# Local attention on one Trainium2 core: inverse norms by refinement steps for two groups at once, and a new table of slots

## The reference

```python
q, k, v = jnp.split(shift_tokens(x) @ Wqkv, 3, -1)      # 16 heads of 64
q = q / jnp.maximum(jnp.linalg.norm(q, axis=-1, keepdims=True), 1e-12) * qs
k = k / jnp.maximum(jnp.linalg.norm(k, axis=-1, keepdims=True), 1e-12) * ksc
q = q * cos * scale + rotate_half(q) * sin * scale
k = k * cos / scale + rotate_half(k) * sin / scale
x = local_attention(q, k, v, window=32) @ Wo + x
x = ffn(shift_tokens(x)) + x                            # layernorm, W1, gelu gate, W2
```

## Time and profile before

| | us |
|---|---|
| median of 3 executions | 4810.02 (4803.85 to 4811.19) |
| the profiled execution | 4799.15 |
| its span | 4797.3 |
| phase B in it | about 512 to 4070 |
| busy, share of the span | PE 88%, DVE 84%, ACT 78%, POOL 73% |

### The profile page before, as it was taken

One profiled execution on the slowest core, in us unless ns is written; L12 is line 12 of the kernel. 1 busy time (PEld: TensorE's weight loads), 2 busy tenths in 40 slices (PEclk: granted clock), 3 DMA queues, 4 the chain that ended last, 5 costly groups with the idle time before them and its releaser, 6 DMA issues. The chain is left out here.

```text
span 4797.3 us, 131407 instructions
## 1 busy us (share of the span) xinstructions
PE 4226.0 (88%) x45166; PEld 3150.4 (66%) x45166; DVE 4007.1 (84%) x7658; ACT 3749.9 (78%) x11543; POOL 3518.3 (73%) x2504
## 2 busy tenths in 40 slices
PE   6988699998999989998889989999899998688887
PEld 3555477776777777776777767777677776354553
DVE  4776798888888888888888888898898895688887
ACT  2555588888888888888888888888888887677774
POOL 0100699988899888998989989899899995344444
PEclk9999799999999999999999999999999999788888
DMA  1000111111111111111111111111121111000000
GB/s 27 6 5 2 49 48 44 44 38 52 53 40 43 48 48 47 44 44 45 46 53 43 40 45 52 47 44 44 45 53 38 44 44 28 3 4 3 3 3 5
DMA packets 118641, 169.38 MB, mean 35 GB/s; under 512 B 26563, under 2 KB 44422, under 8 KB 118022
## 3 DMA queue, kind: packets, MB, share of 16 engines
q1 hardware_dynamic: 109246, 160.92, 12.7%
q10 hardware_dynamic: 8776, 0.45, 0.1%
HBM read 20.79 MB, written 2.10 MB: 5 GB/s over the span
## 5 line engine op out<-in xcount | busy, mean ns | idle before, releaser
L1377 POOL TENSOR_TENSOR b_w<-b_w,b_vt 128x512 f32<-128x512 f32 x768 | 1188.4, 1558 | 331.8 <-DVE b_vt L1289 184.1
L1381 POOL TENSOR_TENSOR b_rn<-b_ssm,all_neg_half 128x16 f32<-128x16 f32 x384 | 1171.7, 3051 | 32.0
L1174 ACT ACTIVATE b_Pr<-ps,b_nm 128x96 f32<-128x96 f32 x3072 | 1002.8, 353 | 3.4 <-DVE b_nm L1346 2.8
L1174 ACT ACTIVATION_READ_ACCUMULATOR b_Pr<-ps,b_nm 128x1 f32 x3072 | 677.1, 220 | 0.0
L1216 ACT ACTIVATE b_PT<-ps 96x512 f32<-96x512 f32 x768 | 458.1, 597 | 264.1 <-PE ps L1026 257.1
L1060 PE MATMUL ps<-b_Whi,b_xlo 128*128 128x512 f32 x1152 | 579.2, 503 | 61.7 <-DVE b_Wlo L1306 25.8
L989 PE MATMUL ps<-all_ident,b_w 128*128 128x128 f32 x3072 | 460.6, 281 | 182.3 <-DVE b_xtok L282 118.7
L1340 DVE TENSOR_TENSOR b_Pr<-b_Pr,b_rinv 128x384 f32<-128x384 f32 x768 | 547.0, 712 | 26.3
L1026 PE MATMUL ps<-all_ident,b_Pr 128*96 128x128 f32 x3072 | 479.2, 279 | 68.8 <-ACT b_PT L1216 47.1
L1287 DVE TENSOR_TENSOR b_w<-ps,until_b_rotab 128x512 f32<-128x512 f32 x768 | 524.0, 682 | 8.9 <-ACT b_sq L1193 5.4
L1346 DVE TENSOR_REDUCE b_nm<-ps 128x8 f32<-128x768 f32 x384 | 367.5, 957 | 190.8 <-PE ps L1015 184.6
(11 more groups left out here) (259 smaller groups left out, 9375.4 us busy)
## 6 DMA issues: line engine op xcount, KB each, us to landing
b_V<-b_Vraw SPq DMA_DIRECT2D x384, 192.0 KB, 2.6
b_V<-b_Vraw SPq DMA_DIRECT2D x384, 128.0 KB, 2.4
b_V<-b_Vraw SPq DMA_DIRECT2D x192, 64.0 KB
b_Wraw<-in_L_ffn_Wqkv SPq DMA_DIRECT2D x36, 256.0 KB, 3.4
b_Wo<-in_L_ffn_Wo SPq DMA_DIRECT2D x6, 512.0 KB, 4.5
a_xtok<-in_L_attn_hidden_states SPq DMA_DIRECT2D x16, 128.0 KB, 2.1
out<-c_xout SPq DMA_DIRECT2D x16, 128.0 KB, 1.8
b_W<-in_L_ffn_W SPq DMA_DIRECT2D x6, 341.0 KB, 3.3
```

What stands on the lines that cost most here:

```text
L1174: last = nc.scalar.activation(s.Pr[:, r % 2, j, i], ps[:, S_BANK[j], i * KEYS:(i + 1) * KEYS], ACT.Exp, bias=s.nm[:, r, j, i:i + 1], accum ...
L1377: nc.gpsimd.tensor_tensor(rows, rows, s.vt[:, i % 4], ALU.add).then_inc(s.pool_add, 1)
L1381: nc.gpsimd.tensor_tensor(s.rn[:, j], s.ssm[:, j], g.neg_half[:, 0:HB], ALU.pow).then_inc(s.pool_r, 1)
```

## The change

What it does:

- The clamp and the power of each group (8 instructions a step on POOL) give way to inverse_root(b), called after add 3 (b = 0, groups 0 and 1) and after add 7 (b = 1, groups 2 and 3). It is a chain of 12 instructions on both groups at once, 128x32 each: clamp and scale, a first guess from the bits of the number as an integer, and two refinement steps. Each waits for the one before it on the semaphore root_step; the last counts pool_r up, once for two groups.
- Both of DVE's groups, 2 and 3, are now normalised within the step (slots 28 and 31), POOL's two at slots 13 and 19. PE's waits for them follow the tables.
- The slots are laid anew: the pieces at 0, 4, 6, 7, 16, 18, 22, 23; ROTATE_LAG is 0 where it was 2; both halves of a round are exponentiated in one slot (lags 4, 4) and scaled in one (5, 5); the moments stand at 20, the last residual at 27, the gate product on POOL at 22.

```diff
-QK_SLOT = {0: (0, 0), 2: (0, 2), 6: (1, 0), 8: (1, 2), 16: (0, 1), 17: (0, 3), 22: (1, 1), 24: (1, 3)}
-ROTATE_LAG, ADD_LAG = 2, 2
+QK_SLOT = {0: (0, 0), 4: (0, 2), 6: (1, 0), 7: (1, 2), 16: (0, 1), 18: (0, 3), 22: (1, 1), 23: (1, 3)}
+ROTATE_LAG, ADD_LAG = 0, 2
...
-DVE_NORM_SLOT = {27: 2}
-DVE_LATE_NORM_SLOT = {4: 3}
-POOL_NORM_SLOT = {7: 0, 16: 1}
+DVE_NORM_SLOT = {28: 2, 31: 3}
+DVE_LATE_NORM_SLOT = {}
+POOL_NORM_SLOT = {13: 1, 19: 0}
...
-                    dve.wait_ge(s.pool_r, 4 * item + j + 1)
+                    dve.wait_ge(s.pool_r, 2 * item + j // 2 + 1)
...
+                def inverse_root(b):
+
+                    done = ROOT_STEPS * (2 * f + b)
+                    js = slice(2 * b, 2 * b + 2)
+                    x, y, t = s.ssm[:, js], s.rn[:, js], s.rt[:]
+                    three, linear, constant = [g.root_c[:, i].rearrange("p (j h) -> p j h", j=2) for i in range(3)]
+                    nc.gpsimd.tensor_scalar(x, s.ss[:, js], 1e-24, ROOT_S, ALU.max, ALU.mult).then_inc(s.root_step, 1)
+                    pool.wait_ge(s.root_step, done + 1)
+                    pool.sem_inc(s.root_step, 1)
+                    nc.gpsimd.tensor_scalar(y.bitcast(I32), x.bitcast(I32), -0.5, ROOT_MAGIC, ALU.mult, ALU.add).then_inc(s.root_step, 1)
+                    pool.wait_ge(s.root_step, done + 3)
+                    nc.gpsimd.tensor_tensor(t, x, y, ALU.mult).then_inc(s.root_step, 1)
+                    pool.wait_ge(s.root_step, done + 4)
+                    nc.gpsimd.tensor_tensor(t, t, y, ALU.mult).then_inc(s.root_step, 1)
...
+                    pool.wait_ge(s.root_step, done + 12)
+                    nc.gpsimd.tensor_tensor(y, t, y, ALU.mult).then_inc(s.pool_r, 1)
...
-                        if c // 2:
-                            nc.gpsimd.tensor_scalar_max(s.ssm[:, j], s.ss[:, j], 1e-24).then_inc(s.clamp_done, 1)
-                            pool.wait_ge(s.clamp_done, 4 * f + j + 1)
-                            nc.gpsimd.tensor_tensor(s.rn[:, j], s.ssm[:, j], g.neg_half[:, 0:HB], ALU.pow).then_inc(s.pool_r, 1)
+                        if i % 4 == 3:
+                            inverse_root(i // 4)
```

More of the change, by code:

```diff
@@ L13 @@
 from contextlib import ExitStack
+import math
 import numpy as np
@@ L22 @@
 F32R = mybir.dt.float32r
+I32 = mybir.dt.int32
 ALU = mybir.AluOpType
@@ L153, in _ @@
             nc.vector.memset(g.neg_half[:], -0.5)
+            for i, value in enumerate(ROOT_C):
+                nc.vector.memset(g.root_c[:, i], value)
             nc.vector.memset(g.minus[:], -1.0)
@@ L1359, in body, with normalise @@
                 f, t, u = step.n + 1, step.n - 1, step.n - 2
+                def normalise(item, j):
+                    pool.wait_ge(s.pool_r, 2 * item + j // 2 + 1)
+                    pool.wait_ge(s.pool_add, N_QK * item + 2 * j + 2)
+                    both = s.w[:, j % 2, j // 2].rearrange("p k (h e) -> p (k h) e", e=DB)
+                    nc.gpsimd.tensor_tensor(both, both, s.rn[:, j].rearrange("p (h o) -> p h o", o=1).broadcast_to((P, HB, DB)),
+                                            ALU.mult).then_inc(s.normed_pool, 1)
@@ new lines, in inverse_root @@
+                def inverse_root(b):
[11 more added lines that the diff above has]
+                    nc.gpsimd.tensor_tensor(t, t, y, ALU.mult).then_inc(s.root_step, 1)
+                    pool.wait_ge(s.root_step, done + 5)
+                    nc.gpsimd.tensor_tensor(t, three, t, ALU.subtract).then_inc(s.root_step, 1)
+                    pool.wait_ge(s.root_step, done + 6)
+                    nc.gpsimd.tensor_tensor(y, t, y, ALU.mult).then_inc(s.root_step, 1)
+                    pool.wait_ge(s.root_step, done + 7)
+                    nc.gpsimd.tensor_tensor(t, x, y, ALU.mult).then_inc(s.root_step, 1)
+                    pool.wait_ge(s.root_step, done + 8)
+                    nc.gpsimd.tensor_tensor(x, t, y, ALU.mult).then_inc(s.root_step, 1)
+                    pool.wait_ge(s.root_step, done + 9)
+                    nc.gpsimd.tensor_tensor(t, x, linear, ALU.subtract).then_inc(s.root_step, 1)
+                    pool.wait_ge(s.root_step, done + 10)
+                    nc.gpsimd.tensor_tensor(t, t, x, ALU.mult).then_inc(s.root_step, 1)
+                    pool.wait_ge(s.root_step, done + 11)
+                    nc.gpsimd.tensor_tensor(t, t, constant, ALU.add).then_inc(s.root_step, 1)
+                    pool.wait_ge(s.root_step, done + 12)
+                    nc.gpsimd.tensor_tensor(y, t, y, ALU.mult).then_inc(s.pool_r, 1)
@@ L1360, in body @@
                 for slot in range(STEP_SLOTS):
                     if step.front is not None and slot in POOL_NORM_SLOT:
[L1362 to L1367, removed]
+                        normalise(f, POOL_NORM_SLOT[slot])
@@ L1368, in body @@
+                    if step.attn and slot in POOL_LATE_NORM_SLOT:
+                        normalise(step.n, POOL_LATE_NORM_SLOT[slot])
                     if step.front is not None and slot - ADD_LAG in QK_SLOT:
```

41 lines of the change are left out of this document (26 added, 15 removed).

## The result

The changed kernel takes 4978.83 us (median of 4 runs, 4977.92 to 4980.03) against 4807.07 of the kernel before on the same chip: ratio 1.0356, 95% interval 1.0344 to 1.0369, 172 us slower. The forecast was slower, 4900, in a range from 4765 to 5015.

The account below looks back on a forecast made before the run. The loop through DVE was taken to set the pace, 35.7 us a step. The new loop, 36.05 + 0.7 = 36.75, adds 1.1 over 84 steps: 92 on 4799, plus 11, gives 4900 us, range 4765 to 5015.

Parts of the forecast that it names:

- The loop: DVE's group 2 product waits for rotate 7, add 7 and the chain: 36.0 or 36.1 us a step, against 35.7.
- under 3 us a step, the chain's links were cheaper: Sign of being wrong: DVE's wait for rn before the product in normalise that small means cheaper links.
- 30.5 us from group 2's product round to the end of rotate 7: DVE's own part of the loop, into the next step: 31.9 - 1.4 = 30.5 us.
- The two extra terms: On top of the loop: waits for round 1's exponentials, 0.5 us a step, and POOL late at rotate 7, 0.2.
- The collisions at 1.4 us: DVE's scalings and products slowed opposite POOL's work: kept at 1.4 us a step, bounds 0.5 and 2.0.
- 84 steps, two at the change of layers swallow it: About two of a layer's 16 steps absorb the loss, leaving 14 x 6 = 84 steps, 92 us.
- What the other moves cost: at nothing: The other moved slots cost nothing, as PE needs 33.1 us of a 36.75 us step.
- worth nothing by itself: POOL's 5.4 us a step less work gains nothing, since others did not wait for POOL.
- The gelu in the way: Gelu at slot 22 on ACT delays rotate 7 in odd steps: up to 84 us more, 4985; chance 0.12.
- The dear chain: POOL's chain takes 5.6 us instead of 4.1: 126 us more, 5025; chance 0.12.
- the integer instruction that costs like a power: In POOL's chain it costs some 5.5 us on 32 columns: 437 us more, 5340; chance 0.04.
- The faster rival: Links of 0.28 us, fewer collisions: 4776 or 4701; decided by chain plus extra terms under 3.7 us; chance 0.2.

Follow-up runs that it names:

- new_slots_product: Changed kernel's slot table without chains, each group's clamp kept and its power replaced by a product, norms not computed: 4875.12 us (1.0146).
- short_second: Changed kernel with only the second chain (groups 2 and 3) cut from twelve to six instructions: 4850.06 us (1.0088).
- chain_alone: Kernel before with its old slots but the two chains; POOL's product for group 0 moves from slot 7 to 12: 5303.51 us (1.1035).
- old_slots_product: Kernel before with its power on POOL replaced by a product of the same shape, norms not computed: 5062.58 us (1.0533).

## Why the prediction was right in its direction and half in its size

**The loop: right.** Its link was to be the product of group 2 waiting for add 7 and the chain. The wait is there once a step, the second chain takes 4.03 against 4.1 (the first, opposite DVE's splits, 4.7), and taking half of it out where it stands in the loop gives back 129 us, against 6 elsewhere. The signature "about 4 us" came as 2.9, since 1.8 of the gap carries PE's name, as the working had said of the last residual. So the sign "under 3 us a step, the chain's links were cheaper" was met and pointed wrong: the links were 0.33, as priced.

**"30.5 us from group 2's product round to the end of rotate 7": mis-sized, and the largest part of the miss.** Measured 31.25 (2074.39 to 2105.64), and 31.66 in the step before it, with the 0.3 for a square in it. It is not that DVE works more, its busy time is the same. The 31.9 it was worked out from subtracts 7.5 us of waits from the pair, and one of the four waits for scores in the earlier trace rows had passed before the pair's window begins, at 2174.74. DVE in the kernel before:

```profile
2172.22 0.56 DVE L1340 TENSOR_TENSOR b_Pr<-b_Pr,b_rinv 128x384 f32<-128x384 f32 x1
2174.38 0.96 DVE L1346 TENSOR_REDUCE b_nm<-ps 128x8 f32<-128x768 f32 x1 [1.60 <-PE ps L1015]
```

The pair itself holds 7.5 - 1.6 = 5.9 us of waits. DVE's own time was thus (71.36 - 5.9)/2 = 32.7 a step, small gaps included, and the loop's term 31.3. The changed kernel gives the same 32.7, worked out with its 9.6 us of waits: (74.95 - 9.6)/2.

**The two extra terms: the sum nearly right, by luck, the shares not.** The exponentials of round 1 were to cost 0.5; DVE waits 1.8 us for them in all of 1000 to 3500, so nothing. POOL was to be 0.2 late; it is 0.5. With these the working reads 31.3 + 1.3 + 0.08 + 4.03 + 0.08 + 0.5 = 37.3, plus 0.15 for the square of piece 23 (0.3 once a pair) 37.4, against 37.47 measured.

**The collisions at 1.4 us: right in sum.** The scaling's mean rose from 710 ns to 745 in 1000 to 3500, the first half of the split from 303 to 688, the product's fell from 1.35 to 1.22, so (8 x 0.185 + 2 x 0.01) is 1.5 a step by the forecast's way of counting; the new meeting of add 1 and the scaling of round 0 that was foreseen takes 1.66 instead of 0.56.

**"84 steps, two at the change of layers swallow it": wrong.** Over one whole layer of 16 steps, before and after (the converting step and the fourth after it beneath):

```profile
1655.25:2246.10 590.85, 538.52 (x6562) 428.56 (x6561) 517.85 (x1031) 506.67 (x1678) 524.38 (x337) 0.99 0.17 46
1655.25:1702.98 47.73, 37.22 (x413) 28.57 (x412) 37.02 (x71) 34.36 (x109) 33.05 (x22) 0.93 0.18 49
1810.53:1852.59 42.06, 36.04 (x413) 28.80 (x412) 32.93 (x65) 31.22 (x103) 33.05 (x23) 0.92 0.23 64
```

```profile
1710.05:2328.06 618.01, 548.34 (x6563) 433.92 (x6560) 518.88 (x1031) 510.54 (x1679) 386.34 (x593) 0.98 0.17 44
1710.05:1760.83 50.78, 37.93 (x411) 29.12 (x408) 37.76 (x72) 33.88 (x109) 24.89 (x39) 0.87 0.17 45
1874.22:1915.73 41.51, 36.96 (x410) 28.81 (x408) 32.91 (x66) 31.19 (x103) 24.17 (x38) 0.92 0.22 61
```

27.2 us a layer, 163 in six. The converting step pays 3.05 itself, and only the one of 42.06 swallows the change. The two errors make the miss on the whole: 92 us were forecast as 84 x 1.1; 96 x 1.1 is 106, and 96 x 0.7 = 67 more for the mis-sized step gives 173, against 172. Why the converting step got longer though DVE came later wasn't tried; the granted clock in it fell from 0.93 to 0.87, and whether that is a cause of it is open.

**"What the other moves cost: at nothing": right for the forecast, too kind on POOL's time.** The cover that was named does hold in the changed kernel, since the chain's wait hides the rest: the last residual is done 2.4 and 3.3 us ahead of rn. What the new order costs with no chain stays open, since the 68 us of new_slots_product have a meeting of POOL and DVE in them that the changed kernel hasn't. And "worth nothing by itself" for POOL's freed time (8.5 us a step in busy time in 1000 to 3500, 5.4 in the forecast, which counted the gaps in the chains) was too kind: in the old order a kernel whose POOL has some 10 us less to do is 256 us slower.

**The rivals.** The gelu in the way is refuted: the square of piece 23 waits 0.3 us in odd steps, and the steps are 37.22 and 37.73. The dear chain is refuted, and so is the integer instruction that costs like a power: 0.22 us. The faster rival is refuted at its first condition, a link of 0.28: it is 0.33. Its point of decision, chain and extra terms under 3.7 us, is refuted too: in short_second the second chain has lost six links of 0.33, so chain and lateness come to some 2.5, and the kernel is still 0.9% slower than before. DVE's own time is 0.8 us a step higher than reckoned, and in every second step of short_second its way to rotate 7 is another 1.5 us longer, mostly by waits for ACT. By the slope of the Trainium skill (GPSIMD Engine Reference, section 3.1) the chain would have taken 2.5 us, an estimate; the trace doesn't agree, with 4.03.

**What fell of my theory.** The loop sets the time of the changed kernel, but it is not DVE's alone. Five rearrangements that were to take the wait off DVE's queue, or hide work in it, lost or gave little (5404, 5301, 5226, 5707, 4932), as other waits took its place. What they share, as I read them, is that groups 2 and 3 are finished last and needed first; pairing them makes group 2 wait for rotate 7. A second cause isn't separated from this: in the four slow ones and in chain_alone the granted clock over the run is 0.90 to 0.93 where it is 0.96 before and after, and PE is busy 35.3 to 36.7 us a step in 1000 to 3500 instead of 34.3, so part of their loss may be slower work on PE. No version beat the kernel before. How much of the 5304 of chain_alone is the phase of POOL against DVE, as in old_slots_product, and how much the waits, stays open; DVE's busy time rose there by 0.6 us a step only, so most is waiting.

## What to carry to other kernels

Batching two groups takes work off an engine (32.7 to 24.2 us a step here) and puts the first group's result behind the second group's last input: before counting the saved work, look where the consumer of the first group stands, and what is queued behind it. Cross-check a time "own = span - waits" against busy time in the same window, and see that each wait lies wholly inside: one that straddled the edge cost this forecast 0.8 us a step. In a tuned order a lighter engine isn't free either; see what its long instruction lay opposite to. The same goes for a stand-in that is to price an order with some work left out: it moves what meets what.

## What the runs showed of the hardware

- A DVE instruction with one SBUF input was held up by POOL as well: in old_slots_product the split of 64x255 (L1241) took 1.98 us for 0.29 and ended 0.15 behind POOL's product. The Trainium skill says so of this kind of instruction (SBUF — State Buffer, "Who interferes with whom"): tensor_scalar can enter a mode that uses the ports shared with GpSimd. The trace agrees, with that 1.98.
- POOL's power did not hold DVE up in the kernel before: splits of 0.30 and 0.29 and a two-input instruction of 0.42 ran within its 3.27 us. The same section has the shared pair held for the whole instruction; for the power the trace doesn't agree.
- On POOL, 128x32 takes 0.25 us with two inputs, 0.22 to 0.28 on integers, and 0.08 passes to the next that waits for it. Where an instruction that only counts a semaphore up stands between, the gap is 0.19.
